# The expert layers of a four-layer network: one stage for everything ahead of the experts, and next-layer weight loads beside the layer before

## What is computed

```python
def _moe_layer(x, rw, rb, g, b, w1, b1, w2, b2):          # E=4 experts, H=128, F=512, K=2
    logits = jnp.einsum('bsh,he->bse', x, rw) + rb
    probs = jax.nn.softmax(logits, axis=-1)
    vals, idx = jax.lax.top_k(probs, K)
    vals = vals / vals.sum(axis=-1, keepdims=True)
    mu = x.mean(axis=-1, keepdims=True)
    xc = x - mu
    xhat = xc * jax.lax.rsqrt((xc * xc).mean(axis=-1, keepdims=True) + EPS)
    xe = xhat[None] * g[:, None, None, :] + b[:, None, None, :]
    h = jax.nn.gelu(jnp.einsum('ebsh,ehf->ebsf', xe, w1) + b1[:, None, None, :], approximate=False)
    y = jnp.einsum('ebsf,efh->ebsh', h, w2) + b2[:, None, None, :]
    expert_out = x[None] + y
    comb = jnp.einsum('bsk,bske->bse', vals, jax.nn.one_hot(idx, E, dtype=x.dtype))
    return jnp.einsum('bse,ebsh->bsh', comb, expert_out)
```

## Time and profile before

| what | value |
|---|---|
| three timed runs | 5080.98, 5087.88, 5090.33 us, median 5087.88 |
| the profiled execution | 5081.71 us, of which the span from first to last instruction is 5080.0 us |
| mean granted TensorE clock | 0.898 of 2.4 GHz |
| busy share of the span | TensorE 85%, VectorE 65%, ScalarE 45%, GpSimd 24% |
| the expert layers | from 2930.59 to 3576.26 us of the span |

### The profile page before, as it was taken

How to read it: one execution, slowest core, us unless ns; L and a number is a source line. 1 busy time by engine, 2 the same in 40 slices (tenths; PEclk the granted TensorE clock), 3 DMA queues, 4 the chain that set the end, 5 groups by cost and what they waited for, 6 DMA issues and landing times. The chain is left out here.

```text
span 5080.0 us, 100345 instructions
## 1 busy us (share of the span) xinstructions
PE 4317.0 (85%) x34185; PEld 3663.3 (72%) x34185; DVE 3323.1 (65%) x6273; ACT 2280.0 (45%) x4584; POOL 1238.1 (24%) x1174
## 2 busy tenths in 40 slices
PE   5399999975699999999999667788699999959684
PEld 4277777764599999899999555566477777747573
DVE  4477777755666666666666466777677777755545
ACT  0066666642233333333333244465266666634341
POOL 0122222222110110111111044565222222214320
PEclk6599999987799999999999877888699999979797
DMA  7345445510101101101101100000255445410382
GB/s 242 96 110 110 107 102 112 113 38 10 47 19 33 24 20 32 24 20 33 24 20 24 44 24 1 0 1 0 57 116 112 106 103 113 110 44 0 79 178 44
DMA packets 190681, 316.83 MB, mean 62 GB/s; under 512 B 132372, under 2 KB 140870, under 8 KB 190406
## 3 DMA queue, kind: packets, MB, share of 16 engines
q1 hardware_dynamic: 186822, 294.71, 25.8%
q10 hardware_dynamic: 3584, 18.43, 0.9%
...
...
## 5 line engine op out<-in xcount | busy, mean ns | idle before, releaser
L1383 ACT ACTIVATE a1m_prob<-a1m_ps_s,a1m_neg_max 128x500 f32<-128x500 f32 x672 | 405.9, 675 | 589.0 <-DVE a1m_neg_max L1319 589.0
L1238 PE MATMUL a1m_ps_o<-a1m_cn,a1m_prob_t 125*128 125x97 f32 x5376 | 633.7, 274 | 0.2 <-issue 0.2
L1238 PEld LDWEIGHTS a1m_ps_o<-a1m_cn,a1m_prob_t 125*128 125x128 f32 x5376 | 620.1, 192 | 0.4 <-issue 0.4
L731 DVE TENSOR_REDUCE a0m_bank_max<-a0m_ps_s 112x1 f32<-112x500 f32 x768 | 488.8, 668 | 150.3 <-PE a0m_ps_s L595 145.2
L731 DVE TENSOR_REDUCE a2m_bank_max<-a2m_ps_s 112x1 f32<-112x500 f32 x768 | 488.7, 668 | 150.4 <-PE a2m_ps_s L595 145.8
L1316 DVE TENSOR_REDUCE a1m_bank_max<-a1m_ps_s 128x1 f32<-128x500 f32 x672 | 455.2, 678 | 173.4 <-PE a1m_ps_s L1204 172.0
L1204 PE MATMUL a1m_ps_s<-a1m_cxt,a1m_qhi 98*128 98x500 f32 x1344 | 441.8, 410 | 24.8 <-issue 18.1
L814 ACT ACTIVATE a0m_prob_t<-a0m_ring 125x448 f32<-125x448 f32 x768 | 391.3, 545 | 95.2 <-PE a0m_ring L549 91.3
L814 ACT ACTIVATE a2m_prob_t<-a2m_ring 125x448 f32<-125x448 f32 x768 | 391.3, 545 | 92.2 <-PE a2m_ring L549 87.9
L1166 POOL TENSOR_TENSOR a1m_cxt<-a1m_raw,g_zeros 98x1500 fp32r<-98x1500 f32 x32 | 86.8, 2711 | 1291.0 <-PE a1m_ps_s L1204 1243.6
L1220 PE MATMUL a1m_ps_t<-g_ident,a1m_prob 128*125 128x128 f32 x2688 | 379.0, 278 | 3.5 <-issue 3.2
...
## 6 DMA issues: line engine op xcount, KB each, us to landing
a0m_ks<-a0m_k_hi SPq DMA_DIRECT2D x256, 187.5 KB
a2m_ks<-a2m_k_hi SPq DMA_DIRECT2D x256, 187.5 KB
a0m_ks<-a0m_k_lo SPq DMA_DIRECT2D x128, 187.5 KB
a2m_ks<-a2m_k_lo SPq DMA_DIRECT2D x128, 187.5 KB
...
```

The source lines that it names most:

```text
L731: dve.tensor_reduce(bank_max[:, h % 2, u, c:c + 1], ps_s[0:ur, c, 0:BK], AX.X, ALU.max).then_inc(maxed, 1)
L1238: m = pe.matmul(ps_o[at, 0:CO], prob_t[:, u % 2, t, at], cn[:, h, t, :], start=(t == 0), stop=(t == KT - 1))
L1383: act.activation(prob[:, s, k * BK:(k + 1) * BK], ps_s[:, k, 0:BK], ACT.Exp, bias=neg_max[:, s:s + 1]).then_inc(exped, 1)
```

## The change

`renorm` loses its `scale` and `raw_t` arguments and gets `plus` (a sum with `hid` and `gs` before the add), `xn`, `xnt` (where to write) and `prefetch` (a list of DMA issues for SP). `logits_of` goes. A new stage `moe_front` holds for one layer what the stages n, l, r and t held, and the split of the weights too; `moe_layer` keeps the chunks alone. In `moe_front` each tile's multiply and add are one `scalar_tensor_tensor`; the logits are matmuls with the router's weights held and 512 columns moving, get their bias on ScalarE as rows of four partitions, and are transposed back by tile; MAX8 and the index searches no longer wait for one another; the gates' high part is made by ScalarE; the weights' high parts are made by ScalarE and the rests by GpSimd. `gwt` is cleared in layer 0 only. The weights of layer 0 are issued in `n3`, those of layer m + 1 in the body of layer m. `n3` writes its normalised rows straight to `hid` and `hid_t`. `m4n` goes; `n4` does its sum.

```diff
-def renorm(nc, g, name, base, addt=None, scale=None, raw_t=None, norm=True):
+def renorm(nc, g, name, base, addt=None, plus=None, norm=True, xn=None, xnt=None, prefetch=None):
+
+    xn, xnt = g.xn if xn is None else xn, g.xnt if xnt is None else xnt
...
+        if prefetch is not None:
+            @block.sync
+            def _(sp):
+                prefetch(sp)
...
-            for n, a, b in groups if raw_t is not None else ():
-                if addt is not None:
-                    pe.wait_ge(based, n + 1)
-                for t in range(a, b):
-                    m = pe.transpose(psb[n][:, t - a, :], base[:, t, :], g.ident[:])
-                m.then_inc(raw_turned, 1)
             for n, a, b in groups if norm else ():
                 pe.wait_ge(normed, n + 1)
-                if raw_t is not None:
-                    pe.wait_ge(raw_kept, n + 1)
                 for t in range(a, b):
-                    m = pe.transpose(psb[n][:, t - a, :], g.xn[:, t, :], g.ident[:])
+                    m = pe.transpose(psb[n][:, t - a, :], xn[:, t, :], g.ident[:])
                 m.then_inc(back, 1)
...
-                if scale is not None:
-                    link(dve.tensor_tensor(v, v, bc(scale, a, b), ALU.mult))
-                if addt is not None:
+                if plus is not None:
+                    hid, gs = plus
                     dve.wait_ge(turned, n + 1)
-                    dve.tensor_tensor(v, v, psa[n][:, 0:b - a, :], ALU.add).then_inc(based, 1)
-                    dve.wait_ge(based, n + 1)
+                    for t in range(a, b):
+                        dve.scalar_tensor_tensor(hid[:, t, :], hid[:, t, :], gs[:, t:t + 1], psa[n][:, t - a, :],
+                                                 ALU.mult, ALU.add).then_inc(mixed, 1)
+                    dve.wait_ge(mixed, b)
+                    link(dve.tensor_tensor(v, v, hid[:, a:b, :], ALU.add))
+                elif addt is not None:
+                    dve.wait_ge(turned, n + 1)
+                    link(dve.tensor_tensor(v, v, psa[n][:, 0:b - a, :], ALU.add))
...
-def logits_of(nc, g, name, xt, experts, w, bias, loaded, out):
...
+def moe_front(nc, g, m, hid, hid_t, gs, rw, rb, router_in, gw, gwt, pick_r, w1, w2, w1s, w2s, loaded):
...
+        @block.tensor
+        def _(pe):
+            def scores(n, a, b):
+
+                if not first:
+                    pe.wait_ge(raw_kept, n + 1)
+                pe.matmul(psa[n][0:ME, 0:(b - a) * P], rw, hid_t[:, a * P:b * P], start=True, stop=True
+                          ).then_inc(scored, 1)
+
+            for n, a, b in groups if not first else ():
+                for t in range(a, b):
+                    r = pe.transpose(psa[n][:, (t - a) * P:(t - a + 1) * P], g.addt[:, t * P:(t + 1) * P], g.ident[:])
+                r.then_inc(turned, 1)
+            pe.wait_ge(router_in, 32)
+            for n, a, b in groups if not first else ():
+                pe.wait_ge(mixed, b)
+                for t in range(a, b):
+                    r = pe.transpose(psb[n][:, t - a, :], hid[:, t, :], g.ident[:])
+                r.then_inc(raw_turned, 1)
+                if n > 0:
+                    scores(*groups[n - 1])
+            for n in (3,) if not first else range(4):
+                scores(*groups[n])
+            for n, a, b in groups:
+                pe.wait_ge(biased, n + 1)
+                for t in range(a, b):
+                    r = pe.transpose(psl[:, t, :], lgt[:, t * P:(t + 1) * P], g.ident[0:ME, 0:ME])
+            r.then_inc(rows_made, 1)
+            for n, a, b in groups:
+                pe.wait_ge(normed, n + 1)
+                for t in range(a, b):
+                    r = pe.transpose(psb[n][:, t - a, :], g.xn[:, t, :], g.ident[:])
+                r.then_inc(back, 1)
+            pe.wait_ge(gated, 1)
+            for n, a, b in groups:
+                for t in range(a, b):
+                    r = pe.transpose(psa[n][0:ME, (t - a) * P:(t - a + 1) * P], gw[:, t, :], g.ident[:])
+                r.then_inc(gate_turned, 1)
+
+        @block.vector
+        def _(dve):
+            link = chain(dve, dved)
+
+            def variance(n, a, b):
+                dve.wait_ge(squared, n + 1)
+                link(dve.tensor_reduce(var[:, a:b], sq[:, a:b, :], AX.X, ALU.add))
+                dve.tensor_scalar(var[:, a:b], var[:, a:b], 1.0 / D, EPS, ALU.mult, ALU.add).then_inc(varred, 1)
+
+            if first:
+                dve.memset(gwt[:].bitcast(F32), 0.0).then_inc(cleared, 1)
+                dve.memset(pick_r[:].bitcast(F32), 0.0).then_inc(cleared, 1)
+            link(dve.memset(v[:], -1.0))
+            for n, a, b in groups:
+                x = hid[:, a:b, :]
+                if not first:
+                    dve.wait_ge(turned, n + 1)
+                    for t in range(a, b):
+                        dve.scalar_tensor_tensor(hid[:, t, :], hid[:, t, :], gs[:, t:t + 1],
+                                                 psa[n][:, (t - a) * P:(t - a + 1) * P], ALU.mult, ALU.add
+                                                 ).then_inc(mixed, 1)
+                    dve.wait_ge(mixed, b)
+                link(dve.tensor_reduce(mu[:, a:b], x, AX.X, ALU.add))
+                link(dve.tensor_scalar(mu[:, a:b], mu[:, a:b], 1.0 / D, None, ALU.mult))
+                dve.tensor_tensor(xc[:, a:b, :], x, bc(mu, a, b), ALU.subtract).then_inc(centred, 1)
+                if n > 0:
+                    variance(*groups[n - 1])
+            variance(*groups[-1])
+            for n, a, b in groups:
+                dve.wait_ge(powed, n + 1)
+                dve.tensor_tensor(g.xn[:, a:b, :], xc[:, a:b, :], bc(rstd, a, b), ALU.mult).then_inc(normed, 1)
+
+            dve.wait_ge(rows_made, 1)
+            link(dve.tensor_reduce(s1[:], psl, AX.X, ALU.max))
+            dve.tensor_tensor(v[:, :, 0:ME], psl, spread(s1[:], ME), ALU.subtract).then_inc(asked, 1)
+            dve.wait_ge(exped, 1)
+            link(dve.tensor_reduce(s1[:], v[:, :, 0:ME], AX.X, ALU.add))
+            link(dve.reciprocal(s1[:], s1[:]))
+            link(dve.tensor_tensor(v[:, :, 0:ME], v[:, :, 0:ME], spread(s1[:], ME), ALU.mult))
+            for t in range(NT):
+                dve.max(top[:, t, :], v[:, t, :]).then_inc(ranked, 1)
+            dve.wait_ge(ranked, NT)
+            for t in range(NT):
+                dve.max_index(idx[:, t, :], top[:, t, :], v[:, t, :]).then_inc(ranked, 1)
+            dve.wait_ge(ranked, 2 * NT)
+            link(dve.tensor_copy(idxf[:], idx[:]))
+            iota = g.iota8[:].rearrange("p (o e) -> p o e", o=1).broadcast_to([P, NT, 8])
+            link(dve.tensor_tensor(h0[:], idxf[:, :, 0:1].broadcast_to([P, NT, 8]), iota, ALU.is_equal))
+            link(dve.tensor_tensor(h1[:], idxf[:, :, 1:2].broadcast_to([P, NT, 8]), iota, ALU.is_equal))
+            link(dve.tensor_tensor(s1[:], top[:, :, 0], top[:, :, 1], ALU.add))
+            link(dve.reciprocal(s1[:], s1[:]))
+            link(dve.tensor_tensor(s2[:], top[:, :, 1], s1[:], ALU.mult))
+            link(dve.tensor_tensor(s1[:], top[:, :, 0], s1[:], ALU.mult))
+            link(dve.tensor_tensor(h0[:], h0[:], spread(s1[:], 8), ALU.mult))
+            link(dve.tensor_tensor(h1[:], h1[:], spread(s2[:], 8), ALU.mult))
+            dve.tensor_tensor(gw[:], h0[:, :, 0:ME], h1[:, :, 0:ME], ALU.add).then_inc(gated, 1)
+            dve.wait_ge(gated, 1)
+            link(dve.tensor_reduce(gs[:], gw[:], AX.X, ALU.add))
+            for n, a, b in groups:
+                dve.wait_ge(gate_high, n + 1)
+                dve.tensor_tensor(gwt[LOW:LOW + ME, a * P:b * P], psa[n][0:ME, 0:(b - a) * P],
+                                  gwt[0:ME, a * P:b * P].bitcast(F32), ALU.subtract).then_inc(gate_low, 1)
+
+        @block.gpsimd
+        def _(pool):
+            for n, a, b in groups:
+                pool.wait_ge(varred, n + 1)
+                pool.tensor_tensor(rstd[:, a:b], var[:, a:b], g.half[:, a:b], ALU.pow).then_inc(powed, 1)
+            for n, (whole, (high, low)) in enumerate(((w1f, w1s), (w2f, w2s))):
+                pool.wait_ge(w_high, n + 1)
+                pool.tensor_tensor(low[:], whole, high[:].bitcast(F32), ALU.subtract).then_inc(w_low, 1)
+
+        @block.scalar
+        def _(act):
+            def high_weights(whole, high):
+                act.wait_ge(loaded, 96)
+                act.activation(high[:], whole, ACT.Copy).then_inc(w_high, 1)
+
+            def bias(n, a, b):
+                act.wait_ge(scored, n + 1)
+                act.activation(lgt[:, a * P:b * P], psa[n][0:ME, 0:(b - a) * P], ACT.Identity, bias=rb
+                               ).then_inc(biased, 1)
+
+            if not first:
+                high_weights(w1f, w1s[0])
+            act.wait_ge(router_in, 32)
+            for n, a, b in groups:
+                if first:
+                    bias(n, a, b)
+                act.wait_ge(centred, n + 1)
```

(72 more changed lines are left out.)

106 lines of the change are left out of this document (39 added, 67 removed).

## The result

The changed kernel takes 4946.05 us, the median of four runs (4944.59 to 4965.12), beside 5089.1 for the kernel before (four runs, 5080.98 to 5091.19). The ratio is 0.9737, with a 95% interval of 0.9720 to 0.9755. Compared again it was 0.9755 (0.9738 to 0.9773; median 4956.52 of five runs). The predicted 4948 us are 0.9725 of the 5087.88 shown before: inside the first interval, a little under the second; both medians lie in the range of 4930 to 4970. The first profiled execution took 4946.81 us, its span is 4945.1.

A forecast was written before the change was run, and what follows sets the result against it. Fronts were taken as bound by a chain hopping between engines over four barriers, with an unhidden load stage before layer 0. Gains of 40.4, 76.0, 18.1 and 3.6 sum to 138.1 us, giving 4948 us, range 4930 to 4970.

The forecast's parts named there:

- load stage: Stage of DMA issues before layer 0: gone, its 7.9 us of issue hidden in n3, a gain of 40.4 us.
- fronts of layers 1 to 3: From the last body's end to the next body's first matmul: 34.9 us each, a gain of 76.0 us together.
- front of layer 0: From the stage's start to its body's first matmul: 54.99 us falls to 36.9, a gain of 18.1 us.
- end, m4n in n4: The 7.59 us stage summing the last layer goes and n4 gets 4.0 us of instructions: a gain of 3.6 us.
- the race for the ports: Layers 1 to 3: VectorE's last normalisation goes before GpSimd's first weight subtraction, which then runs from 15.8 to 20.5 us.
- case (a): Rival: GpSimd wins the ports at the last normalisation, gates 4.3 us later three times, 4961 us; chance 0.17.
- the searches: Router on VectorE, 14 MAX8 and 14 index searches without waits: 4.5 us instead of 6.7, bounds 3.9 and 6.7.
- the multiply: Router on VectorE: under rival GpSimd-first, it waits for the second weight split, to 25.2 us from the front's start.
- Ready rows: Layers 1 to 3, logits transposed back by TensorE: ready at 18.3 us from the front's start; wrong if later than 19.
- (b): Rival: small router instructions on VectorE do not wait for GpSimd's subtractions, 4940 us; chance 0.14.
- (c): Rival: the load isn't hidden and n3 is held open as long as the old stage, 4988 us; chance 0.05.
- (d): Rival: slower than before, bodies staying at 1.2 GHz, 80 us a body, 5028 to 5268 us; chance 0.02.

The follow-up runs named there:

- e4: The changed kernel with the load issues of all four layers in n3 and none in the bodies: median 4980.3 us, ratio 0.9808 to the kernel before.
- e5: The kernel before with only the loads moved, layer 0's into n3 and each later layer's into the expert stage before it: median 5034.1 us, ratio 0.9919.
- c1: The changed kernel as it is, compared again with the kernel before: median 4956.5 us, ratio 0.9755.
- e3: The changed kernel with its 28 search instructions chained again, each waiting for the one before: median 4964.8 us, ratio 0.9764 to the kernel before.
- e8: The changed kernel with GpSimd's two rests cut into eight pieces of 512 columns: median 4942.9 us, ratio 0.9728 to the kernel before.
- e1: The changed kernel without GpSimd's two rests in layers 1 to 3, which changes the computation: median 4941.6 us, ratio 0.9722 to the kernel before.
- e2: The changed kernel with GpSimd beginning its rests only when all four groups of rows are normalised: median 4949.3 us, ratio 0.9736 to the kernel before.
- e6: The changed kernel with both rests on VectorE, w1's behind the gates and w2's in the body: median 4941.0 us, ratio 0.9703 to the kernel before.

## Why the prediction held, step by step

The difference of the two profiled spans is 5080.0 - 4945.1 = 134.9 us; the prediction's sum was 138.1. Its terms:

| term | predicted gain | measured gain |
|---|---|---|
| load stage | 40.4 | 40.4 |
| fronts of layers 1 to 3 | 76.0 | 68.7 |
| front of layer 0 | 18.1 | 19.1 |
| end, m4n in n4 | 3.6 | 3.0 (24.68 to 21.68) |
| bodies | 0 | 0.5 (402.4 to 402.0) |
| outside | 0 | 3.2 (the rest of the program varies by 17) |

**Load.** Right, and for the reason given: e4 and e5 show both sides of it. The issues themselves took 11.9 us in n3, not 7.9, a figure read from rows in which they went out in another order: the bias load b1 took 4.05 us behind w2 and had taken 0.51 behind w1 (no run changed the order alone). The 17.0 of n3 covered it.

**Layer 0.** Right in mechanism: first rest at 17.7 us from its start (18.2), index conversion held to its end, the comparison behind it held to the second's end at 26.7 (27.8), gates at 28.9 (30.2), first matmul at 35.89 (36.9).

**Layers 1 to 3.** Here a step failed: "VectorE's instruction just before started 0.02 us after GpSimd's earlier one had ended, and went first", the argument by which the race for the ports was given to VectorE. GpSimd won it in all three layers, and in all twelve of the four other runs with this order (c1, e3, e4, e8). By the trace GpSimd's next instruction comes right behind its own power, 0.06 us ahead of VectorE's, which has to hear of that power's end first. In the earlier trace rows neither waited for the other: VectorE's cast came next in its own queue, and it took 0.39 us, as it did at 1325.03 with GpSimd idle. (That this decides is argued from the starts; no run moved them by a tenth of a microsecond.) So case (a), put at 0.17, is the one that happened. It was to cost 4.3 us in each of three layers; it cost 2.2 to 2.7, since two terms of the sum were mis-sized:

- the searches were put at 4.5 us and took 3.1 (3052.46 to 3055.55), under even the lower bound of 3.9. An unchained MAX8 costs 0.075 us, an index search 0.14. With the race lost they are on the path, so all of it counts;
- the multiply was free at 24.4 us from the start and not at 25.2, since a rest takes 4.50 to 4.68 us and starts at 15.2, not 15.4. The gates came at 30.2 (30.6 in layer 2) and not at 32.4.

On the profiled execution case (a) would have been 4943.6 + 12.9 = 4956.5. Less 5.6 in these three fronts (68.7 us gained, and that case gives 76.0 - 12.9 = 63.1), less 1.0 in layer 0, plus 0.6 at the end, less 0.5 and 3.2 in bodies and the rest of the program: 4946.8, which it took. The closeness to 4948 is thus owed in part to luck, to terms that offset one another.

Ready rows came at 14.4 us (15.8 in layer 2), not 18.3. The 14 transposes from four partitions took 1.02 us in layers 1 and 3, where the granted clock was 1.00 in them, and 1.65 in layer 2, where it was 0.50:

```profile
3179.76 1.65 PE L1922 MATMUL m2n_psa<-g_ident,m2n_lgt 4*128 4x4 f32 x14
```

3.6 were predicted, priced by one 15.57 us stage at 0.50 that had other instructions in it, so the price was the larger error and the clock the smaller. A 512-column fp32 matmul took 1.87 us at 0.50, near the 1.75 predicted from a row of another stage, and 1.02 at 1.00; the forecast had taken fronts that stay at 0.50, and these had 0.65 to 0.68 on the whole. It changed nothing, for VectorE stood in its normalisation until 19.9. The worry that the exponent waits on ScalarE's high part was void in the changed kernel for the same reason, and came true in e1, e2 and e6, where the wait was 1.36 us.

In e2, where the race goes as forecast, the fronts are 34.2 to 34.6 against 34.9: the sum was good to 0.7 us. There the index conversion waits for the second rest, which ends at 24.7 us from the start in layer 1, not at 25.5. The searches, 1.4 us shorter than forecast, lie under that rest, and the later exponent under the first, so neither counts.

**What no run takes alone** is the merging of the four stages and the new form of the logits. Of layer 1's 24.0 us (61.18 to 37.15), e3 shows 3.6 to be the searches; the logits stage had taken 15.57 by itself, and the new logits are ready before VectorE can use them. The other 4.9 are a remainder, of the barriers and the mixed instructions less what the lock costs.

**The other rivals.** (b) fell: small instructions do stand, 3.22 us for a 56-element multiply. The Trainium skill (SBUF — State Buffer, "SBUF: two separate sides"), whose rule is the exclusive lock for a whole instruction, agrees with the trace. (c) did not occur, but e4 shows that it would have with all the loads in one stage. (d) did not occur: the bodies show 0.97 to 0.98 on the whole, as before (6.00 us at 0.50 and 94.24 at 1.00 make 0.97), out of fronts that were less cold than before, 0.55 to 0.68 beside 0.50 to 0.57.
